# Where the maxima's transposition and VectorE's residual and norms stand among the scores

## What is computed

```python
scores = jnp.einsum('bhtd,bhsd->bhts', q, k) / jnp.sqrt(HD)
probs = jax.nn.softmax(scores, axis=-1)
attn = jnp.einsum('bhts,bhsd->bhtd', probs, v)
...
x = _layernorm(x + attn)                       # the residual
...
nodes[c] = act_w[c] * o + q                    # six nodes
...
out = (z - mu) * rsqrt(var + 1e-6) * g + b     # first final norm
x = _layernorm(x + out)                        # second final norm
```

## Time and profile before

| | us |
|---|---|
| median of 3 runs | 2220.38 |
| lowest, highest | 2218.78, 2220.67 |
| the profiled execution | 2223.95 |
| its span | 2221.9 |
| TensorE busy | 2039.9 (92%) |
| VectorE busy | 1737.5 (78%) |
| ScalarE busy | 1486.8 (67%) |
| GpSimd busy | 341.7 (15%) |

### The profile page before, as it was taken

The page is one execution under the profiler, slowest core; times in us unless marked ns, Lnnn a source line. Parts: engine busy times, 40 slices in busy tenths (PEclk is TensorE's granted clock), DMA queues, the critical chain, the costliest instruction groups (busy, mean ns, idle before and its releaser), DMA issues.

```text
span 2221.9 us, 32029 instructions
## 1 busy us (share of the span) xinstructions
PE 2039.9 (92%) x10812; PEld 846.9 (38%) x10812; DVE 1737.5 (78%) x3501; ACT 1486.8 (67%) x2004; POOL 341.7 (15%) x385
## 2 busy tenths in 40 slices
PE   5748886999999999999999999999999999999995
PEld 2224443333333333444444444444444444443332
DVE  5856887788787877888888888888878888888884
ACT  4743453566666677777777777777777777776664
POOL 1101332000000011111111111111111111113223
PEclk9977786799999999999999999999999999999998
DMA  3001104233333355566566656556666566665630
GB/s 103 19 24 54 56 33 86 43 66 75 63 75 67 82 104 107 117 109 109 109 109 109 108 109 109 108 110 109 109 110 108 108 109 109 109 108 101 98 58 25
DMA packets 137197, 195.63 MB, mean 88 GB/s; under 512 B 20152, under 2 KB 55632, under 8 KB 137040
## 3 DMA queue, kind: packets, MB, share of 16 engines
q1 hardware_dynamic: 137040, 193.63, 45.5%
HBM read 75.45 MB, written 23.73 MB: 45 GB/s over the span
## 4 chain that ended last, share of the span: by engine, by line
PE 81%; DVE 13%; issue 4%; ACT 1%; POOL 1%; DMA 1%; DVEq 0%; POOLq 0%; SPq 0%; ACTq 0%
PE bank_s L1031 27%; PE bank_o L1069 22%; PE bank_x L1054 6%; DVE nm L1386 5%; PE bank_m L1082 3%; PE bank_x L1017 3%; PE bank_x L996 3%; PE bank_x L1004 2%; PE bank_m L1102 2%; PE bank_x L983 2%; PE bank_x L1128 2%; PE bank_s L934 1%; DVE big L1275 1%; PE bank_m L1092 1%; PE bank_m L1041 1%
## 5 line engine op out<-in xcount | busy, mean ns | idle before, releaser
L1386 DVE TENSOR_REDUCE nm<-bank_s 128x1 f32<-128x512 f32 x2048 | 1336.2, 685 | 342.3 <-PE bank_s L1031 341.4
L821 ACT ACTIVATE big<-bank_x 128x1024 f32<-128x1024 f32 x1024 | 1048.0, 1024 | 486.5 <-PE bank_x L1054 458.9
L1031 PE MATMUL bank_s<-kst,qst 62*128 62x512 f32 x2048 | 837.5, 469 | 53.1 <-DVE nm L1386 52.5
L1054 PE MATMUL bank_x<-qst,kst 64*128 64x512 f32 x2048 | 750.0, 447 | 1.6 <-ACT big L821 1.6
L1031 PEld LDWEIGHTS bank_s<-kst,qst 62*128 62x128 f32 x2048 | 358.9, 187 | 693.3 <-DVE nm L1386 609.4
L1069 PE MATMUL bank_o<-big,at 128*32 128x512 f32 x4096 | 556.4, 616 | 2.2 <-ACT big L821 2.0
L1054 PEld LDWEIGHTS bank_x<-qst,kst 64*128 64x128 f32 x2048 | 304.3, 187 | 10.2 <-issue 6.0
L605 POOL CAST at<-at 128x512 fp32r<-128x512 f32 x112 | 68.2, 609 | 1273.3 <-ACT at L752 1035.8
L607 POOL TENSOR_TENSOR at<-at 128x512 fp32r<-128x512 f32 x112 | 143.3, 1280 | 10.0
L1069 PEld LDWEIGHTS bank_o<-big,at 128*32 128x32 f32 x4096 | 81.2, 108 | 153.1 <-issue 149.2
L829 ACT ACTIVATE big<-bank_x,big 128x128 f32<-128x128 f32 x256 | 68.7, 376 | 27.3 <-issue 11.6
(11 more groups left out here) (154 smaller groups left out, 1511.4 us busy)
## 6 DMA issues: line engine op xcount, KB each, us to landing
at<-nodes_d SPq DMA_DIRECT2D x144, 256.0 KB, 5.9
kst<-at SPq DMA_DIRECT2D x288, 128.0 KB
qst<-at SPq DMA_DIRECT2D x288, 128.0 KB
nodes_d<-big SPq DMA_DIRECT2D x48, 256.0 KB, 3.1
at<-w_d SPq DMA_DIRECT2D x48, 193.0 KB, 5.8
at<-x2T_d SPq DMA_DIRECT2D x32, 256.0 KB, 4.4
kst<-at SPq DMA_DIRECT2D x128, 64.0 KB
qst<-at SPq DMA_DIRECT2D x128, 64.0 KB
```

The lines of the kernel that those rows point to most:

```text
L821: act.activation(PT[:, kp, h, :, :], ring.take()[0].rearrange("p (c n) -> p c n", c=2), ACT.Exp, scale=x.c.scale).then_inc(S["c_ex"], 1)
L1031: pe.matmul(bank_s[:, n % 2, :], qst[rows, x.r, h, t * P:(t + 1) * P], kst[rows, x.r, h, :], start=True, stop=True).then_inc(S["c_s_ps"], 1)
L1054: mm = pe.matmul(sec(to, j), kst[rows, x.r, h, kc_ * P:(kc_ + 1) * P], qst[rows, x.r, h, :], start=True, stop=True)
L1386: dve.tensor_reduce(nm[:, k, at_n:at_n + 1], bank_s[:, n % 2, :], AX.X, ALU.max, negate=True).then_inc(S["c_red"], 1)
```

## The change

It moves work within the units and changes how two pieces are cut.

- `maxima` and `ev_m` go from step 1 to the end of step 2, behind the projection and its copy; `parts` goes from step 6 to step 7.
- The residual is done in single pieces, each after one maximum: the sum, four statistics, the aggregation and four normalisations, at the places of `RESIDUAL_AT`.
- So are the final norms. Their first normalisation goes from 1.5 of the unit after to 0.0 and 0.1 of the unit after that, the second statistics to 0.5 to 0.7, the second normalisation to 1.1 and 1.2.
- On GpSimd the multiplication and the sum move one unit later with it, and the offset's addition goes ahead of the root.
- For the last unit VectorE does the gain and the sum itself (`final_gain`), in eight operations with two inputs.
- SyncE issues the first of the maxima's DMAs ahead of the store of a result.

```diff
+RESIDUAL_AT = [(0, 5, 0), (0, 5, 1), (0, 6, 0), (0, 6, 1), (0, 7, 0), (0, 7, 1), (1, 1, 0), (1, 1, 1), (1, 2, 0), (1, 2, 1)]
+FIRST_NORM_AT = [(1, 3, 0), (1, 3, 1), (1, 5, 0), (1, 5, 1), (1, 6, 1)]
+SECOND_NORM_AT = [(0, 0, 0), (0, 0, 1), (0, 1, 0), (0, 1, 1), None,
+                  (0, 5, 0), (0, 5, 1), (0, 6, 0), (0, 6, 1), (0, 7, 0),
+                  (1, 1, 0), (1, 1, 1), (1, 2, 0), (1, 2, 1)]
...
@@ sync
                 load_x3(at_(c, q, r - 1))
-                store_out(at_(c, q, r - 2))
                 ahead, nxt = at_(c, q, r + 3), at_(c, q, r + 1)
                 rows_m(nxt, 0)
+                store_out(at_(c, q, r - 2))
...
@@ gpsimd
+            def final_rstd(x):
...
-                rstd(mv, rs0, rs, eps_node[:, :], (S["f_mv"], j + 1), (S["f_rs_link"], j + 1), S["f_rs"])
                 need(pool, S["f_x3_in"], 16 * (j + 1))
                 pool.tensor_tensor(x33, x33, b3, ALU.add).then_inc(S["f_plink"], 1)
+                rstd(mv, rs0, rs, eps_node[:, :], (S["f_mv"], j + 1), (S["f_rs_link"], j + 1), S["f_rs"])
...
             def body(c, q, r):
                 residual_rstd(at_(c, q, r - 1))
-                final_sum(at_(c, q, r - 1))
+                final_sum(at_(c, q, r - 2))
+                final_rstd2(at_(c, q, r - 2))
+                final_rstd(at_(c, q, r - 1))
                 split(at_(c, q, r + 3))
-                final_rstd(at_(c, q, r - 1))
...
@@ scalar
-                        if i == 1:
-                            ev_m(*led_group(c, q, r, k))
                         if k == 0:
                             if i == 2:
                                 ev_v(at_(c, q, r + 1))
+                                ev_m(*led_group(c, q, r, k))
...
                             if i == 2:
                                 ev_qT(ahead)
                                 ev_kh(only(ahead, False))
+                                ev_m(*led_group(c, q, r, k))
...
@@ tensor
-                        if i == 1:
-                            maxima(*led_group(c, q, r, k))
...
                             if i == 2:
                                 value(at_(c, q, r + 1))
+                                maxima(*led_group(c, q, r, k))
...
                                 proj_kh(only(ahead, False))
+                                maxima(*led_group(c, q, r, k))
...
@@ vector
+            def final_gain(x):
+
+                j = final(x)
+                need(dve, S["f_mv"], j + 1)
+                need(dve, S["f_y"], j)
+                for t in range(NT):
+                    cols = slice(t * D, (t + 1) * D)
+                    dve.scalar_tensor_tensor(zn[:, cols], nT[:, cols], mv[:, t, 0:1], lngb[:, 0, :],
+                                             ALU.subtract, ALU.mult).then_inc(S["f_gain"], 1)
+                need(dve, S["f_rs"], j + 1)
+                need(dve, S["f_plink"], 2 * j + 1)
+                need(dve, S["f_gain"], NT)
+                for t in range(NT):
+                    cols = slice(t * D, (t + 1) * D)
+                    i = dve.scalar_tensor_tensor(zn[:, cols], zn[:, cols], rs[:, t:t + 1], x2s[:, cols], ALU.mult, ALU.add)
+                i.then_inc(S["f_z"], 1)
...
-                            if i == 6:
+                            if i == 7:
                                 parts(*read_group(c, q, r, k), j)
...
+                            at_step = k, i, j
+                            if at_step in RESIDUAL_AT:
+                                residual(last, RESIDUAL_AT.index(at_step))
+                            if at_step == (1, 0, 1):
+                                node_out(last)
+                            if at_step in FIRST_NORM_AT:
+                                final_norm(last, FIRST_NORM_AT.index(at_step))
+                            if at_step in SECOND_NORM_AT:
+                                final_norm(at_(c, q, r - 2), NT + 1 + SECOND_NORM_AT.index(at_step))
...
             node_out(end)
-            for step in range(4):
+            for step in range(NT + 1):
+                final_norm(end, step)
+            final_gain(end)
+            for step in range(2 * (NT + 1), 4 * (NT + 1)):
                 final_norm(end, step)
```

More of the change, by code:

```diff
@@ L231, in build @@
               "link", "link2", "link3")
-        names("f_", "x3_in", "tT_ps", "tT_ev", "mv", "rs", "rs_link", "nm", "z", "mv2", "rs2", "rs2_link", "y", "out", "link", "link2", "plink")
+        names("f_", "gain", "x3_in", "tT_ps", "tT_ev", "mv", "rs", "rs_link", "nm", "z", "mv2", "rs2", "rs2_link", "y", "out", "link", "link2", "plink")
         names("c_", "qk0", "qk1", "v0", "v1", "o0", "o1", "kh_ps", "qh_ps", "qT_ps", "v_ps", "ot_ps", "mT_ps", "wo_ps", "cT_ps", "x3T_ps",
@@ L675, in body @@
                 residual_rstd(at_(c, q, r - 1))
-                final_sum(at_(c, q, r - 1))
+                final_sum(at_(c, q, r - 2))
+                final_rstd2(at_(c, q, r - 2))
+                final_rstd(at_(c, q, r - 1))
                 split(at_(c, q, r + 3))
-                final_rstd(at_(c, q, r - 1))
             units(pool, body)
-            end = at_(kn, QU - 1, RING - 1)
-            final_sum(end)
+            end, last = at_(kn, QU - 1, RING - 1), at_(kn, QU - 1, RING - 2)
+            final_sum(last)
+            final_rstd2(last)
             final_rstd(end)
+            final_rstd2(end)
         @block.scalar
@@ L1529, in residual @@
                     return
-                for t in {1: (0, 1), 2: (2, 3)}.get(step, ()):
+                if 1 <= step <= NT:
+                    t = step - 1
                     need(dve, S["c_xlink"], base + 1)
                     dve.bn_stats(stt[:, t, :], ctx_sb[:, t * D:(t + 1) * D]).then_inc(S["c_xlink"], 1)
-                if step == 3:
+                if step == NT + 1:
                     need(dve, S["c_xlink"], base + 1 + NT)
@@ L1537, in residual @@
                     i.then_inc(S["c_mv"], 1)
-                if step >= 4:
-                    t = step - 4
+                if step >= NT + 2:
+                    t = step - NT - 2
                     need(dve, S["c_rs"], x.b + 1)
@@ L1552, in final_norm @@
                     return
-                if step == 0:
+                part, t = step // (NT + 1), step % (NT + 1)
+                cols = slice(t * D, (t + 1) * D)
+                if part == 0 and t < NT:
                     need(dve, S["f_tT_ev"], j + 1)
-                    stats(nT, stt, mv, S["f_link"], NT * j, S["f_mv"])
-                if step == 1:
+                    dve.bn_stats(stt[:, t, :], nT[:, cols]).then_inc(S["f_link"], 1)
+                if part == 0 and t == NT:
+                    need(dve, S["f_link"], NT * (j + 1))
+                    for t in range(NT):
+                        i = dve.bn_aggr(mv[:, t, :], stt[:, t, :])
+                    i.then_inc(S["f_mv"], 1)
@@ L1557, in final_norm @@
+                if part == 1 and t < NT:
                     need(dve, S["f_rs"], j + 1)
                     need(dve, S["f_y"], j)
-                    normalise(zn, nT, mv, rs, S["f_nm"])
-                if step == 2:
+                    i = dve.tensor_scalar(zn[:, cols], nT[:, cols], mv[:, t, 0:1], rs[:, t:t + 1], ALU.subtract, ALU.mult)
+                    if t == NT - 1:
+                        i.then_inc(S["f_nm"], 1)
+                if part == 2 and t < NT:
                     need(dve, S["f_z"], j + 1)
-                    stats(zn, stt2, mv2, S["f_link2"], NT * j, S["f_mv2"])
@@ L1563, in final_norm @@
-                if step == 3:
+                    dve.bn_stats(stt2[:, t, :], zn[:, cols]).then_inc(S["f_link2"], 1)
+                if part == 2 and t == NT:
+                    need(dve, S["f_link2"], NT * (j + 1))
+                    for t in range(NT):
+                        i = dve.bn_aggr(mv2[:, t, :], stt2[:, t, :])
+                    i.then_inc(S["f_mv2"], 1)
+                if part == 3 and t < NT:
                     need(dve, S["f_rs2"], j + 1)
                     need(dve, S["f_out"], 16 * j)
-                    normalise(x3s, zn, mv2, rs2, S["f_y"])
+                    i = dve.tensor_scalar(x3s[:, cols], zn[:, cols], mv2[:, t, 0:1], rs2[:, t:t + 1], ALU.subtract, ALU.mult)
+                    if t == NT - 1:
+                        i.then_inc(S["f_y"], 1)
@@ L1586, in body @@
                             reduce(*group)
[L1588 removed]
+                            if i == 7:
                                 parts(*read_group(c, q, r, k), j)
[L1590 to L1602 removed]
+                            at_step = k, i, j
[7 more added lines that the diff above has]
+                                final_norm(at_(c, q, r - 2), NT + 1 + SECOND_NORM_AT.index(at_step))
             units(dve, body)
             end, last = at_(kn, QU - 1, RING - 1), at_(kn, QU - 1, RING - 2)
[L1605 removed]
+            for step in range(NT + 1, 3 * (NT + 1)):
+                final_norm(last, step)
             for step in range(2):
                 divide(end, 1, step)
[L1608 removed]
```

(6 more changed lines are left out.)

23 lines of the change are left out of this document (5 added, 18 removed).

## The result

| | before | after |
|---|---|---|
| median, us | 2219.94 (7 runs) | 2233.15 (7 runs) |
| lowest, highest | 2217.99, 2220.67 | 2227.58, 2240.68 |
| ratio, 95% interval | | 1.0062, 1.0045 to 1.0078 |
| profiled execution, its span | 2223.95, 2221.9 | 2227.58, 2225.8 |

The account below looks back on a forecast made before the run. TensorE was taken to set the pace, with VectorE holding it up. The terms 3.3 - 2.4 - 6.9 - 3.6 - 1.6 - 3.3 = -14.5 us took the median from 2220.4 to 2206, own range 2201 to 2211 (80%: 2194 to 2215).

Parts of the forecast that it names:

- `maxima` behind projections: Node units: step 2's second score tile waits for a maximum delayed by `node_out`, +0.07 in each of 47, +3.3 us.
- `parts` one step later: Node units: the cast leaves 0.6, so `out_proj` in 0.7 starts 0.05 sooner, 47 times, -2.4 us.
- both in the first kind: First-kind units: moving `maxima` and `parts` was taken to change nothing there, 0.
- residual in pieces: First kind: normalisations at 1.1 and 1.2 run before GpSimd's split and aren't held, -6.9 us (-4 to -9).
- final norms, clock there: Final units: VectorE time saved less newly held normalisations, -3.6 us, plus -1.6 us for less half clock.
- tail: After the last unit: offset added earlier, four VectorE operations beside the root and four behind, -3.3 us (gain 2.0 to 4.0).
- in 1.6 nothing is, as TensorE waits there for the projections' copies: Node units, k = 1: moving `parts` out of 1.6 was taken to win nothing, so no term.
- the second rival: Final units: GpSimd holds all four normalisations, 1.2 each, so the final part gives +1 instead of -5.2: 2212 us, 15%.
- The first rival: Some 126 halves: `turn` waits for a late `ev_m` on ScalarE, 0.2 paid in each, 25 us: 2231 us, 8%.
- "Nothing below zero": Moving `maxima` behind the projections can't gain: no TensorE gap the order could fill, but for 0.1 that VectorE's maxima cover.
- The gain of 0.05 in 0.7: Node units, k = 0: with `parts` out of 0.6, `out_proj` starts 0.05 us sooner in 0.7.
- the allowance of 4 us either way: Half-clock stretches, mostly in the first kind, may shift with unit lengths: three at 1.3 us, nothing in the sum.

Follow-up runs that it names:

- parts_back: The changed kernel with `parts` alone back in step 6: 2222.78 us, ratio 1.0017.
- pieces_only: The changed kernel with `maxima` and `ev_m` back in step 1 and `parts` back in step 6, pieces kept: 2215.67 us, ratio 0.9995.
- maxima_back: The changed kernel with `maxima` and `ev_m` alone back in step 1, `parts` still in step 7: 2232.64 us, ratio 1.0049.
- parts_k0: pieces_only with `parts` in step 7 in the first half (k = 0) alone: 2213.5 us, ratio 0.9966.
- late_final: parts_k0 with final first normalisations at 0.2 and 0.5, second statistics at 1.1 and 1.2, second normalisations at 1.6 and 1.7: 2207.61 us, ratio 0.9945.
- old_sums: parts_k0 with the residual's sum and statistics placed as in the kernel before: 2210.42 us, ratio 0.9954.
- maxima_ahead: pieces_only with `maxima` and `ev_m` in step 2, ahead of the projection and its copy: 2197.27 us (1 run).
- before_ahead: The kernel before with `maxima` and `ev_m` in step 2 ahead of the projection, nothing else: 2202.23 us, ratio 0.991.
- copy64: The kernel before with one 128 x 64 VectorE copy ahead of step 1.4's first maximum: 2232.37 us (1 run).
- copy128: The kernel before with one 128 x 128 VectorE copy ahead of step 1.4's first maximum: 2231.76 us (1 run).

## Why the prediction was wrong

| term of the sum | forecast | measured | from |
|---|---|---|---|
| `maxima` behind projections | +3.3 | +10.2 | units 16 to 56, parts_back against pieces_only |
| `parts` one step later | -2.4 | +11.1 | units 16 to 56, maxima_back against pieces_only |
| both in the first kind | 0 | -1.6 | 446.2 in after, 444.2 in pieces_only, less 8.9 us of low clock at 0.41 |
| residual in pieces | -6.9 | -7.5 | 455.3 to 444.2 in pieces_only, less 8.9 us of low clock at 0.41 |
| final norms, clock there | -5.2 | -0.2 | 205.1 to 206.3 in pieces_only, less 3.4 us of low clock at 0.41 |
| tail | -3.3 | -3.8 | 27.0 to 23.2 |
| sum | -14.5 | +8.2 | the stretches: +7.2; the medians, with the clock: +13.2 |

The 0.41 is a measured price: parts_k0 and pieces_only have the same operations in the first kind but for the place of `parts` in k = 0, and took 460.3 and 444.2 us with 72.1 and 32.5 us at the low clock, 16.1 / 39.6. late_final, with the same operations there as parts_k0, bears it out: 453.5 us with 55.0. The rows of the table are taken at one clock by it.

**The step that failed** is "in 1.6 nothing is, as TensorE waits there for the projections' copies". I looked at what the cast delays in the place it leaves, and for the new place only at TensorE. I did not ask what GpSimd does in 1.7. The split of the unit three ahead starts there in every node unit, and my own text had it: I counted the held cast of the earlier trace rows among what the final units would save, and held normalisations in the second rival, for those units alone. The row was read as a matter of the final norms, while its mechanism is one of place. It is also the larger part: of the 22.7 us between -14.5 and +8.2, `parts` is 13.5, `maxima` 6.9 less the 1.6 in the first kind, and the final norms 5.0. Without the cost of `parts` the sum is -2.9 by the measured terms, still far from -14.5.

**`maxima` behind the projections** was right in its two mechanisms, and both terms were mis-sized. The late second tile of 1.2 was forecast at 0.07 late and is just that (0.41 less 0.34), but it costs 0.17. I priced the tile's start and not what comes behind it. The same rows give it with the 0.48 from above: the maximum's end at 1231.55 plus 0.48 is 1232.03, and the projection would have come at 1231.19 + 0.66 = 1231.85, so 0.18. `turn` starts when `ev_m` is through, as said; I took the slack of 0.29 at the reciprocal as cover for all of it. The reciprocal is not what is short: the second tile of 1.5 waits for the maxima behind it. They end 0.16 later there and 0.10 in 0.5, and 1.5 is 0.17 longer, 0.5 is 0.11. In k = 0 the 0.21 won in 0.1 is paid back in 0.2 to 0.5; in k = 1 0.21 is won and 0.16 (1.2), 0.12 (1.3 and 1.4) and 0.17 (1.5) are paid. The first rival ("the turn waits for ScalarE") had the right mechanism, at 25 us, and I held it at 8%. "Nothing below zero" was wrong too: the same move ahead of the projection gives -0.27 a unit. In the first kind, where I took nothing, the two moves together gave 1.6.

**The gain of 0.05 in 0.7** does not exist: parts_k0 has the pitch of pieces_only to 0.01.

**Residual:** right. No L1560 is over 0.34 (the L1543 of the forecast), a pair is 53.6 us (27.8 and 25.8) in after and 53.9 in pieces_only where I said 54.0. The term of -6.9 measured -7.5. Steps 1.4 and 1.5 of the unit with a residual went from 4.84 to 3.51, -1.33 for the -1.25; 0.6 to 1.0 from 5.18 to 5.48, +0.30 for the +0.15.

**Final norms:** by its size the part came out near the second rival (+1), though not by its condition: not all four are held. In units 58 to 61 it is the first two of four, 0.31 and 1.05 in unit 58, as I took it, and what was mis-sized is what they cost: steps 0.1 and 0.2 of unit 58 take 5.12 us against 3.77 before, +1.35, where I had +1.0. What the pieces won there is near the forecast: 1.4, 1.5 and 1.7 take 5.71 instead of 7.45, -1.74 where I had -1.9. But 1.3 is 0.25 longer, as is every 1.3 behind the late `turn`. I had 30.2 for a final unit and they are 30.8. The clock's -1.6 is not told apart: after has 3.4 us at the low clock there where before has 6.8, which is worth 1.4, but pieces_only, parts_back and maxima_back have 10.2. late_final puts a size on it, with the other places in it: 28.9 to 29.2.

**Tail:** right, 3.63 from root to statistics. The eight operations take 1.19 and 1.14 a four, within my 0.8 to 1.4, and the first four are not held by the root (1.19 beside it, 1.14 without), so the rule of the Trainium skill (SBUF — State Buffer, Who interferes with whom) by which the gain would be 2.8 is not borne out for this pair; GpSimd's operation there has 128 x 4 elements.

**Clock:** the allowance of 4 us either way was too small for this kernel. Before's runs keep within 3 to 8 us of each other in each session, the one of 4242.08 aside. Those of pieces_only go from 2205.08 at a mean granted clock of 0.952 to 2231.46 at 0.938, and the stretches at half clock of the profiled runs in the first kind sum to 32.5 us there, 41.4 in before and after, 72.1 in parts_k0, 75.5 in maxima_back. Taken at one clock the parts agree with the table. At 0.952, where the last digit is worth some 2 us: pieces_only 2205.1, parts_back 2216.6 and 2217.4, after 2227.6, before about 2218. So the pieces gave some 12.5 us, `maxima` took 12, `parts` 10.5, and after is some 9.5 behind before. These rest on one or two runs each. Why the runs of before keep to one pattern of such stretches and those of the pieces don't stays open: the eleven runs of old_sums lie within 15 us, the five of parts_k0 within 17, the twelve of pieces_only within 27.

## What to carry to other kernels

Before a VectorE operation in SBUF is moved, however small, look at what GpSimd does in the step it goes to: a subtraction of 16 columns cost 0.84 us instead of 0.17 there. When something is inserted or delayed, follow it to the maxima behind it and to what TensorE starts after the tile that needs them (here 0.48 us behind the maximum's end), and don't stop at the slack of the one instruction that waits, nor at the tile's recorded start. Where a short transposition can stand on either side of a projection, put it ahead, so that its copy is through before the next user of the bank asks.

## What the runs showed of the hardware

- The transposition of `mp` (128 x 32) took 0.21 us of TensorE's list ahead of a score tile, 0.13 ahead of a projection (maxima_ahead), and 0.20 behind one. With it ahead, the whole kernel was 18 us faster than before (before_ahead) with the same instructions.
- The work of TensorE behind the second score tile started 0.48 us after the end of the maximum that this tile waits for, and at the soonest 0.66 behind the first tile (before, after, copy64, copy128). The first 0.10 of a delay stood in the second tile's recorded length, 0.50 instead of 0.39, and not in its start.
- A cast and a subtraction of 128 x 16 on VectorE, 0.17 each, took 0.45 and 0.84 beside GpSimd's split and ended 0.03 and 0.02 behind its operations (after; 0.17 again in parts_back).
- A VectorE copy of 128 x 64 or 128 x 128 in a full row of operations cost TensorE 0.03 and 0.06 us, and one of 128 x 4 nothing.
- The mean granted clock of the same program differs from run to run by up to 0.014, and the time with it by 26 us (pieces_only).
